# Splitting each scan step of a Mamba block into two halves of eight states

## The chip, the cores and the metric

The kernel runs on all 8 NeuronCores of one Trainium2 chip, each with two of the sixteen sequences. The time is that of the slowest core, in microseconds of the device, for one execution of the whole kernel. Lower is better.

## What is computed

A selective state-space (Mamba) block with a residual and a LayerNorm, and then a feed-forward block with a low-rank, token-dependent term, again with residual and LayerNorm. Model width is 1024, inner width 2048, 16 states for each inner channel, 2048 tokens in each sequence. The part that the change touches is the recurrence over the tokens:

```python
delta = softplus(xp[..., -1:] * w_dt + b_dt)
dA  = exp(delta[..., None] * A)                    # b, l, 2048, 16
dBx = (delta * xc)[..., None] * B_in[:, :, None, :]
def step(h, inp):
    dA_t, dBx_t, C_t = inp
    h = dA_t * h + dBx_t
    return h, einsum('bdn,bn->bd', h, C_t)         # y_t
y = ys + D_param * xc
y = y * silu(z)
return y @ W_out.T
```

## The kernel before

The kernel has three stages behind one another, with a barrier between them. The first casts and transposes the weights into scratch memory. The second, the scan phase, goes through 16 chunks of T = 256 tokens (8 for each of the core's two sequences). The third is the feed-forward block.

In the scan phase the 2048 inner channels are 16 groups of 128 partitions, and one group is a *step* here, counted 0 to 15 by `dt` in a chunk. The 16 states lie side by side in a row, so `dA`, `dbx` and `hc` are tiles of 128 x 4096 (16 states x 256 tokens). One scan instruction runs over several states in one go: the first column of `dA` of each state is set to zero, so that nothing is carried from one state into the next, and what the chunk before leaves over (`scar`) is put in by adding `dA * scar` to the first column of `dbx` (through `fixb`). In the first chunk of a sequence (k = 0) this pair of instructions is left out.

ScalarE (`emit_dA`, L702) makes `dA` with 16 `Exp` activations of 256 columns and then signals `dA_{jd}`. There are two `dA` buffers, and before it fills one it waits for `scan_{jd - 2}`. Its program is in one written-out order: behind step 0's `dA` the LayerNorm statistics of the chunk before; behind steps 2 to 5 four copies each of transposed input (L648) for the next chunk; behind steps 6 to 12 five or four evacuations each (`prep_evac`, L663 and L671), which wait for TensorE's products for the next chunk; ahead of step 8 the second half of `delta` (L693, L697); behind step 13 the evacuation of the B/C projection.

GpSimd multiplies `delta` by `xc` into `vv`, eight groups at a time (`vhalf`, L540), and signals `vH_{i}_{h}`, for which VectorE waits at steps 0 and 8. It also issues the chunk's loads and stores of its own queue. TensorE works on the next chunk's input projection and then on the output projection of the chunk before (`emit_wout_kt`), slab by slab as `ybuf` comes.

VectorE's step is a chain: wait for `dA`, `dbx` = `vv` x `brep` (L764), `fixb` (L772), add (L778), memset (L782), two scans over half of the row each (L786, L788) of which the second signals `scan_{jd}`, copy of the last column (L793), product with C (`crep`, L797), four adds that fold 16 states into one (L799 to L805), and the two instructions that make `ybuf` (L807, L811). Between instructions that depend on each other stands a `drain`. At the start of each chunk VectorE adds and normalizes the chunk before (L394, L412).

Of the kernel before, what the change touches and what calls it, by code (L numbers as in the profile page):

```python
# [8 lines left out]
FP16 = mybir.dt.float16  # L9
BF16 = mybir.dt.bfloat16  # L10
AF = mybir.ActivationFunctionType
OP = mybir.AluOpType

P = 128
# [4 lines left out]
NST = 16  # L19
H = 4096  # L20
T = 256
NCH = L // T
NDT = DIN // P
# [42 lines left out]
def build_nc(known_events=None, n_iters=B_LOC * NCH, do_a=True, do_b=True):  # L66
# [27 lines left out]
    ev = Ev(nc, known=known_events)  # L94
# [3 lines left out]
    a_sb = nc.alloc_sbuf_tensor("a_sb", [P, NDT * NST], F32)  # L98
# [238 lines left out]
    tsb = lambda nm, sh, dt: stA.enter_context(nc.sbuf_tensor(nm, sh, dt))  # L337
# [8 lines left out]
    vv = [tsb(f"vv{j}", [P, NDT * T], BF16) for j in range(2)]  # L346
    brep = [tsb(f"brep{j}", [P, NST * T], BF16) for j in range(2)]
    crep = [tsb(f"crep{j}", [P, NST * T], BF16) for j in range(2)]
    dtrep = [tsb(f"dtrep{j}", [P, T], F32) for j in range(2)]
    delta = [tsb(f"delta{j}", [P, T], F32) for j in range(8)]  # L350
    dA = [tsb(f"dA{j}", [P, NST * T], FP16) for j in range(2)]
    dbx = [tsb(f"dbx{j}", [P, NST * T], BF16) for j in range(2)]
    hc = tsb("hc", [P, NST * T], BF16)
    fixb = tsb("fixb", [P, NST], F32)
    scar = tsb("scar", [P, NDT * NST], F32)
# [10 lines left out]
    def it_bk(i):  # L366
        return i // NCH, i % NCH
# [88 lines left out]
    with nc.Block() as blk:  # L456
# [168 lines left out]
        def _(s):  # L625
# [74 lines left out]
                ev.mark(f"deltaH_{i}_{h}", "ac")  # L700

            def emit_dA(i, dt):  # L702
                jd = i * NDT + dt
                da_t = dA[jd % 2]
                if jd >= 2:
                    ev.wait(s, f"scan_{jd - 2}")
                for n in range(NST):
                    jx = s.activation(da_t[:, n * T:(n + 1) * T], delta[dt % 8][:],  # L708
                                      AF.Exp,
                                      scale=a_sb[:, dt * NST + n:dt * NST + n + 1])  # L710
                jx = ev.inc(jx, "ac", 1)
                ev.mark(f"dA_{jd}", "ac")

            if n_iters > 0:
                prep_tails(0)
# [33 lines left out]
        @blk.vector  # L749
        def _(v):  # L750
            ev.wait(v, "p0_params")
            for i in range(n_iters):
                b, k = it_bk(i)
                par = i % 2
                if i > 0:
                    emit_ln1_evac(v, i - 1)
                    emit_ln1_norm(v, i - 1)
                for dt in range(NDT):
                    if dt % 8 == 0:
                        ev.wait(v, f"vH_{i}_{dt // 8}")  # L760
                        ev.wait(v, f"zsil_{i}_{dt // 8 * 8 + 7}")
                    jd = i * NDT + dt
                    ev.wait(v, f"dA_{jd}")
                    jx = v.tensor_tensor(  # L764
                        dbx[jd % 2][:].rearrange("p (n t) -> p n t", n=NST),
                        vv[par][:, dt * T:(dt + 1) * T].unsqueeze(1)
                        .broadcast_to([P, NST, T]),
                        brep[par][:].rearrange("p (n t) -> p n t", n=NST),
                        OP.mult)
                    v.drain()  # L770
                    if k > 0:
                        jx = v.tensor_tensor(  # L772
                            fixb[:],
                            dA[jd % 2][:].rearrange("p (n t) -> p n t", n=NST)[:, :, 0],
                            scar[:, dt * NST:(dt + 1) * NST],
                            OP.mult)
                        v.drain()
                        jx = v.tensor_tensor(  # L778
                            dbx[jd % 2][:].rearrange("p (n t) -> p n t", n=NST)[:, :, 0],
                            dbx[jd % 2][:].rearrange("p (n t) -> p n t", n=NST)[:, :, 0],  # L780
                            fixb[:], OP.add)
                    jx = v.memset(dA[jd % 2][:]  # L782
                                  .rearrange("p (n t) -> p n t", n=NST)[:, :, 0:1], 0.0)
                    v.drain()
                    HT = NST * T // 2
                    jx = v.tensor_tensor_scan(hc[:, 0:HT], dA[jd % 2][:, 0:HT],  # L786
                                              dbx[jd % 2][:, 0:HT], 0.0, OP.mult, OP.add)
                    jx = v.tensor_tensor_scan(hc[:, HT:], dA[jd % 2][:, HT:],  # L788
                                              dbx[jd % 2][:, HT:], 0.0, OP.mult, OP.add)
                    jx = ev.inc(jx, "vc", 1)  # L790
                    ev.mark(f"scan_{jd}", "vc")
                    v.drain()  # L792
                    jx = v.tensor_copy(  # L793
                        scar[:, dt * NST:(dt + 1) * NST],
                        hc[:].rearrange("p (n t) -> p n t", n=NST)[:, :, T - 1])
                    v.drain()
                    jx = v.tensor_tensor(hc[:], hc[:], crep[par][:], OP.mult)  # L797
                    v.drain()
                    jx = v.tensor_add(hc[:, 0:8 * T], hc[:, 0:8 * T], hc[:, 8 * T:16 * T])  # L799
                    v.drain()  # L800
                    jx = v.tensor_add(hc[:, 0:4 * T], hc[:, 0:4 * T], hc[:, 4 * T:8 * T])  # L801
                    v.drain()
                    jx = v.tensor_add(hc[:, 0:2 * T], hc[:, 0:2 * T], hc[:, 2 * T:4 * T])
                    v.drain()
                    jx = v.tensor_add(hc[:, 0:T], hc[:, 0:T], hc[:, T:2 * T])  # L805
                    v.drain()
                    jx = v.scalar_tensor_tensor(gtmp[:], xc[par][:, dt * T:(dt + 1) * T],  # L807
                                                dp_sb[:, dt:dt + 1], hc[:, 0:T],
                                                OP.mult, OP.add)
                    v.drain()  # L810
                    jx = v.tensor_tensor(ybuf[par][:, dt * T:(dt + 1) * T], gtmp[:],  # L811
                                         zsil[par][:, dt * T:(dt + 1) * T], OP.mult)
                    jx = ev.inc(jx, "vc", 1)
                    ev.mark(f"ydt_{i}_{dt}", "vc")
                    v.drain()
                ev.mark(f"dloop_{i}", "vc")
            if n_iters > 0:
                emit_ln1_evac(v, n_iters - 1)
                emit_ln1_norm(v, n_iters - 1)
# [351 lines left out]
```

How the kernel before makes its waits and increments, by code:

```python
    def wait(self, eng, ev_name):  # L55
        tbl = self.known if self.known is not None else self.events
        if ev_name not in tbl:
            if self.known is not None:
                raise KeyError(f"unknown event {ev_name}")
            return
        sname, val = tbl[ev_name]
        if val > 0:
            eng.wait_ge(self.sem(sname), val)
# [183 lines left out]
            @blk.gpsimd  # L247
# [10 lines left out]
                            else:  # L258
                                ptag = JOBS[[jj[0] for jj in JOBS].index(tag) - 1][0]
                                if ptag == "ws":
                                    ev.wait(g, f"ws_sc{15 - (1 - r)}")
                                else:
                                    ev.wait(g, f"{ptag}_tr{(_prev_nr[ptag]) - (2 - r)}")
                        i = g.dma_start(out=wrow[r % 2][:, 0:cols],
                                        in_=src_ap[r * P:(r + 1) * P, :])
                        ev.inc(i, f"gw{r % 2}", 16)
                        ev.mark(f"{tag}_ld{r}", f"gw{r % 2}")
                g.wait_ge(ev.sem("gw0"), ev.cnt["gw0"])
                g.wait_ge(ev.sem("gw1"), ev.cnt["gw1"])
# [44 lines left out]
            @blk.sync  # L314
# [14 lines left out]
                    ev.mark(f"{tag}_alldoneA", "hd0")  # L329
                    ev.mark(f"{tag}_alldoneB", "hd1")
                sy.wait_ge(ev.sem("hd0"), ev.cnt["hd0"])
                sy.wait_ge(ev.sem("hd1"), ev.cnt["hd1"])
```

## Time and profile before

| | us |
|---|---|
| median of the timed runs (7847.22 and 7870.45) | 7858.83 |
| the profiled execution | 7886.68 |
| its span on the slowest core (core 2) | 7884.8 |
| spans of its eight cores | 7727.9 to 7884.8 |
| VectorE busy | 4727.9 |
| ScalarE busy | 3217.6 |
| TensorE matmul busy | 3936.6 |

All rows below are of core 2. The page of the profile gives the busy time of each engine (PE is TensorE, DVE is VectorE, ACT is ScalarE, POOL is GpSimd), and groups of instructions by line of the kernel. A row of a timeline gives the start in us from the span's start, the duration in us, the engine, the line, what is written from what, and in brackets how long the engine was idle just before and what ended that. "Issue" means that nothing in the profile ended it. A name with q behind the engine (POOLq) is that engine's sequencer.

### The profile page before, as it was taken

The numbers are of one execution on the slowest core, as the hardware profiler recorded it, in microseconds if no ns is written. First come the engines' busy times: TensorE is split into PE (matmuls) and PEld (weight loads), VectorE is DVE, ScalarE is ACT, GpSimd is POOL, SyncE is SP. The second block draws the span as 40 slices with busy tenths as digits, with TensorE's granted clock in tenths as the row PEclk, the third lists the DMA queues.
The fourth block names the chain that finished last, engine by engine and source line by source line (L and its number), as shares of the span: only waits on it lengthen the run. The fifth ranks groups of instructions, "written<-read, shape, count | busy, mean of one in ns | idle before, by whom it ended". The sixth has DMA issues, their size and how long they took to land.

```text
span 7884.8 us, 65714 instructions; the slowest of 8 cores (7727.9 to 7884.8 us)
## 1 busy us (share of the span) xinstructions
PE 3936.6 (50%) x18593; PEld 1984.5 (25%) x18720; DVE 4727.9 (60%) x3817; ACT 3217.6 (41%) x8279; POOL 474.9 (6%) x514
## 2 busy tenths in 40 slices
PE   4445353252542634426335263352500888868888
PEld 2213232131231412304223132131300222222223
DVE  1000488898889888898889898889986000000000
ACT  4443354554545545445455454554531222222221
POOL 0010010000100001000100010000101000010000
PEclk9999676575665666656656566565655777877777
DMA  3576242232322423224233242232303222333332
GB/s 82 112 125 153 82 129 83 68 109 68 108 87 64 119 69 100 88 59 130 77 83 98 58 129 76 75 99 62 115 16 56 77 79 85 96 82 102 102 96 91
DMA packets 591422, 707.86 MB, mean 90 GB/s; under 512 B 421359, under 2 KB 421359, under 8 KB 552160
## 3 DMA queue, kind: packets, MB, share of 16 engines
q1 hardware_dynamic: 561024, 608.48, 25.3%
q0 software_dynamic: 30048, 95.17, 6.7%
q8 instruction: 164, 2.69, 0.1%
q14 instruction: 186, 1.52, 0.1%
HBM read 707.33 MB, written 71.84 MB: 99 GB/s over the span
## 4 chain that ended last, share of the span: by engine, by line
DVE 28%; PE 24%; ACT 14%; DVEq 12%; DMA 7%; issue 4%; another core or an unknown queue 1%; ACTq 1%; POOL 0%; POOLq 0%; SPq 0%
DVE hc L786 11%; DVEq L792 11%; ACT dA L708 8%; PE ps_xz L586 7%; PE ps_h L974 7%; DVE dbx L764 6%; PE ps_oB L1006 5%; DVE hc L797 4%; DMA w1s_r<-win1s_scr 3%; DMA w_r<-w2T_scr 3%; DVE hc L799 2%; DVE hc L801 1%; PE ps_h L977 1%; ACT y1T L1043 1%
## 5 line engine op out<-in xcount | busy, mean ns | idle before, releaser
L708 ACT ACTIVATE dA<-delta,a_sb 128x256 f16<-128x256 f32 x4096 | 1662.2, 494 | 1234.0 <-DVE hc L788 1229.0
L586 PE MATMUL ps_xz<-xT,w1s_r 128*128 128x256 bf16 x8192 | 1154.2, 310 | 340.6 <-ACT xc L663 230.0
L786 DVE TENSOR_TENSOR_SCAN hc<-dA,dbx 128x2048 bf16<-128x2048 f16 x256 | 1132.8, 4425 | 19.5 <-issue 1.0
L788 DVE TENSOR_TENSOR_SCAN hc<-dA,dbx 128x2048 bf16<-128x2048 f16 x256 | 1133.0, 4426 | 0.0
L764 DVE TENSOR_TENSOR dbx<-vv,brep 128x4096 bf16<-128x4096 bf16 x256 | 586.9, 2293 | 836.6 <-ACT dA L708 784.6
L586 PEld LDWEIGHTS ps_xz<-xT,w1s_r 128*128 128x128 bf16 x8192 | 882.3, 110 | 580.1 <-issue 370.7
L379 PE MATMUL ps_wo<-wout_r,ybuf 128*128 128x512 bf16 x993 | 413.9, 568 | 1126.2 <-DVE ybuf L811 823.7
L571 PE MATMUL ps_tr<-ident,x_bf 128*128 128x128 bf16 x256 | 68.0, 266 | 1295.5 <-ACT xT L648 944.0
L602 PE MATMUL ps_xz<-xT,win_r 128*128 128x256 bf16 x2048 | 428.9, 390 | 410.1 <-ACT zsil L671 233.2
L797 DVE TENSOR_TENSOR hc<-hc,crep 128x4096 bf16<-128x4096 bf16 x256 | 592.9, 2316 | 20.8 <-issue 2.1
L1006 PE MATMUL ps_oB<-w_r,h_sb 128*128 128x512 bf16 x2000 | 551.9, 428 | 57.8 <-DMA w_r<-w2T_scr 37.7
L974 PE MATMUL ps_h<-y1T,w1t_sb 128*128 128x512 bf16 x2000 | 554.6, 424 | 16.3 <-DVE su_sb L1092 11.7
L540 POOL TENSOR_TENSOR vv<-delta,xc 128x256 bf16<-128x256 f32 x256 | 317.4, 1271 | 2787.8 <-ACT delta L697 2787.8
L379 PEld LDWEIGHTS ps_wo<-wout_r,ybuf 128*128 128x128 bf16 x1024 | 108.8, 121 | 1422.5 <-issue 1418.3
L1097 DVE TENSOR_SCALAR su_sb<-ps_ut,scl_sb 4x512 bf16<-4x512 f32 x32 | 23.6, 738 | 715.0 <-PE ps_ut L987 715.0
L1126 DVE TENSOR_TENSOR y2pre<-ps_oB,y1cb 128x512 f32<-128x512 f32 x64 | 44.3, 692 | 636.2 <-PE ps_oB L1022 634.4
L602 PEld LDWEIGHTS ps_xz<-xT,win_r 128*128 128x128 bf16 x2048 | 259.2, 133 | 574.4 <-issue 476.5
L663 ACT ACTIVATE xc<-ps_xz 128x256 bf16<-128x256 f32 x256 | 94.1, 382 | 751.0 <-PE ps_xz L590 750.4
L571 PEld LDWEIGHTS ps_tr<-ident,x_bf 128*128 128x128 bf16 x256 | 26.7, 104 | 1347.0 <-issue 1347.0
L1052 ACT ACTIVATE h_sb<-ps_h,b_sb 128x512 bf16<-128x512 f32 x256 | 175.9, 687 | 437.7 <-PE ps_h L977 437.4
L799 DVE TENSOR_TENSOR hc<-hc 128x2048 bf16<-128x2048 bf16 x256 | 320.8, 1253 | 19.4 <-issue 0.4
L307 ACT COPY p_stage<-p_psa 128x128 bf16<-128x128 bf16 x704 | 186.6, 265 | 340.5 <-PE p_psa L241 318.0
(115 smaller groups left out, 3844.0 us busy)
## 6 DMA issues: line engine op xcount, KB each, us to landing
w1s_r<-win1s_scr SPq DMA_DIRECT2D x256, 1024.0 KB, 5.0
w_r<-w2T_scr SPq DMA_DIRECT2D x512, 256.0 KB, 3.1
win_r<-winT_scr SPq DMA_DIRECT2D x256, 256.0 KB, 2.9
wout_r<-woutT_scr SPq DMA_DIRECT2D x256, 256.0 KB, 3.3
win1s_scr<-p_stage SPq DMA_DIRECT2D x64, 256.0 KB, 2.4
brep<-bc_scr POOLq DMA_DIRECT2D x16, 1024.0 KB, 9.4
crep<-bc_scr POOLq DMA_DIRECT2D x16, 1024.0 KB, 14.0
out<-outsb SPq DMA_DIRECT2D x32, 512.0 KB, 4.0
```

The lines of the kernel that those rows point to most:

```text
L379: jx = t.matmul(ps_wo[grp][:], ybuf[par][:, kt * T + tM * P:kt * T + (tM + 1) * P], wout_ring[jj % 2][:, nh * 512:(nh + 1) * 512], start=( ...
L586: jx = t.matmul(pst[:], w1s_ring[jj % 2][:, (k4 * NKD + kt) * P:(k4 * NKD + kt + 1) * P], xT[par][:, kt * TE + 1 + k4:kt * TE + 1 + k4 + T ...
L602: jx = t.matmul(pst[:], win_ring[jj % 2][:, kt * P:(kt + 1) * P], xT[par][:, kt * TE + 4:kt * TE + 4 + T], start=(kt == 0), stop=(kt == NK ...
L708: jx = s.activation(da_t[:, n * T:(n + 1) * T], delta[dt % 8][:], AF.Exp, scale=a_sb[:, dt * NST + n:dt * NST + n + 1])
L764: jx = v.tensor_tensor(dbx[jd % 2][:].rearrange("p (n t) -> p n t", n=NST), vv[par][:, dt * T:(dt + 1) * T].unsqueeze(1) .broadcast_to([P, ...
L786: jx = v.tensor_tensor_scan(hc[:, 0:HT], dA[jd % 2][:, 0:HT], dbx[jd % 2][:, 0:HT], 0.0, OP.mult, OP.add)
L788: jx = v.tensor_tensor_scan(hc[:, HT:], dA[jd % 2][:, HT:], dbx[jd % 2][:, HT:], 0.0, OP.mult, OP.add)
L792: v.drain()
L797: jx = v.tensor_tensor(hc[:], hc[:], crep[par][:], OP.mult)
L799: jx = v.tensor_add(hc[:, 0:8 * T], hc[:, 0:8 * T], hc[:, 8 * T:16 * T])
L974: jx = t.matmul(pst[:], w1t_sb[:, kt * H + m * P:kt * H + (m + 1) * P], y1T[par][:, kt * TB:(kt + 1) * TB], start=(kt == 0), stop=False)
L1006: jx = t.matmul(ps_o[gq][:], h_sb[:, kt * TB + tM * P:kt * TB + (tM + 1) * P], w2_ring[jj % 4][:, nh * 512:(nh + 1) * 512], start=(kt == 0 ...
```

## The change

The tiles `dA` and `dbx` become half as wide (8 states, 128 x 2048) and twice as many (4 instead of 2). ScalarE signals after each eight activations, and waits before each half for the scan that last read the same buffer. VectorE runs the part of the step from `dbx` to the scan twice, once for each half, each with a wait of its own for its half of `dA` and a signal behind its scan. The part of the step from the copy of the last column on stays as it is, on the whole row of `hc`.

```diff
--- before.py
+++ after.py
@@ -348,8 +348,8 @@
     crep = [tsb(f"crep{j}", [P, NST * T], BF16) for j in range(2)]
     dtrep = [tsb(f"dtrep{j}", [P, T], F32) for j in range(2)]
     delta = [tsb(f"delta{j}", [P, T], F32) for j in range(8)]
-    dA = [tsb(f"dA{j}", [P, NST * T], FP16) for j in range(2)]
-    dbx = [tsb(f"dbx{j}", [P, NST * T], BF16) for j in range(2)]
+    dA = [tsb(f"dA{j}", [P, 8 * T], FP16) for j in range(4)]
+    dbx = [tsb(f"dbx{j}", [P, 8 * T], BF16) for j in range(4)]
     hc = tsb("hc", [P, NST * T], BF16)
     fixb = tsb("fixb", [P, NST], F32)
     scar = tsb("scar", [P, NDT * NST], F32)
@@ -700,16 +700,18 @@
                 ev.mark(f"deltaH_{i}_{h}", "ac")
 
             def emit_dA(i, dt):
-                jd = i * NDT + dt
-                da_t = dA[jd % 2]
-                if jd >= 2:
-                    ev.wait(s, f"scan_{jd - 2}")
-                for n in range(NST):
-                    jx = s.activation(da_t[:, n * T:(n + 1) * T], delta[dt % 8][:],
-                                      AF.Exp,
-                                      scale=a_sb[:, dt * NST + n:dt * NST + n + 1])
-                jx = ev.inc(jx, "ac", 1)
-                ev.mark(f"dA_{jd}", "ac")
+                for nh in range(2):
+                    jh = (i * NDT + dt) * 2 + nh
+                    da_t = dA[jh % 4]
+                    if jh >= 4:
+                        ev.wait(s, f"scan_{jh - 4}")
+                    for n8 in range(8):
+                        n = nh * 8 + n8
+                        jx = s.activation(da_t[:, n8 * T:(n8 + 1) * T], delta[dt % 8][:],
+                                          AF.Exp,
+                                          scale=a_sb[:, dt * NST + n:dt * NST + n + 1])
+                    jx = ev.inc(jx, "ac", 1)
+                    ev.mark(f"dA_{jh}", "ac")
 
             if n_iters > 0:
                 prep_tails(0)
@@ -759,37 +761,38 @@
                     if dt % 8 == 0:
                         ev.wait(v, f"vH_{i}_{dt // 8}")
                         ev.wait(v, f"zsil_{i}_{dt // 8 * 8 + 7}")
-                    jd = i * NDT + dt
-                    ev.wait(v, f"dA_{jd}")
-                    jx = v.tensor_tensor(
-                        dbx[jd % 2][:].rearrange("p (n t) -> p n t", n=NST),
-                        vv[par][:, dt * T:(dt + 1) * T].unsqueeze(1)
-                        .broadcast_to([P, NST, T]),
-                        brep[par][:].rearrange("p (n t) -> p n t", n=NST),
-                        OP.mult)
-                    v.drain()
-                    if k > 0:
+                    jh0 = (i * NDT + dt) * 2
+                    for nh in range(2):
+                        jh = jh0 + nh
+                        ev.wait(v, f"dA_{jh}")
                         jx = v.tensor_tensor(
-                            fixb[:],
-                            dA[jd % 2][:].rearrange("p (n t) -> p n t", n=NST)[:, :, 0],
-                            scar[:, dt * NST:(dt + 1) * NST],
+                            dbx[jh % 4][:].rearrange("p (n t) -> p n t", n=8),
+                            vv[par][:, dt * T:(dt + 1) * T].unsqueeze(1)
+                            .broadcast_to([P, 8, T]),
+                            brep[par][:, nh * 8 * T:(nh + 1) * 8 * T]
+                            .rearrange("p (n t) -> p n t", n=8),
                             OP.mult)
                         v.drain()
-                        jx = v.tensor_tensor(
-                            dbx[jd % 2][:].rearrange("p (n t) -> p n t", n=NST)[:, :, 0],
-                            dbx[jd % 2][:].rearrange("p (n t) -> p n t", n=NST)[:, :, 0],
-                            fixb[:], OP.add)
-                    jx = v.memset(dA[jd % 2][:]
-                                  .rearrange("p (n t) -> p n t", n=NST)[:, :, 0:1], 0.0)
-                    v.drain()
-                    HT = NST * T // 2
-                    jx = v.tensor_tensor_scan(hc[:, 0:HT], dA[jd % 2][:, 0:HT],
-                                              dbx[jd % 2][:, 0:HT], 0.0, OP.mult, OP.add)
-                    jx = v.tensor_tensor_scan(hc[:, HT:], dA[jd % 2][:, HT:],
-                                              dbx[jd % 2][:, HT:], 0.0, OP.mult, OP.add)
-                    jx = ev.inc(jx, "vc", 1)
-                    ev.mark(f"scan_{jd}", "vc")
-                    v.drain()
+                        if k > 0:
+                            jx = v.tensor_tensor(
+                                fixb[:, nh * 8:nh * 8 + 8],
+                                dA[jh % 4][:].rearrange("p (n t) -> p n t", n=8)[:, :, 0],
+                                scar[:, dt * NST + nh * 8:dt * NST + nh * 8 + 8],
+                                OP.mult)
+                            v.drain()
+                            jx = v.tensor_tensor(
+                                dbx[jh % 4][:].rearrange("p (n t) -> p n t", n=8)[:, :, 0],
+                                dbx[jh % 4][:].rearrange("p (n t) -> p n t", n=8)[:, :, 0],
+                                fixb[:, nh * 8:nh * 8 + 8], OP.add)
+                        jx = v.memset(dA[jh % 4][:]
+                                      .rearrange("p (n t) -> p n t", n=8)[:, :, 0:1], 0.0)
+                        v.drain()
+                        jx = v.tensor_tensor_scan(hc[:, nh * 8 * T:(nh + 1) * 8 * T],
+                                                  dA[jh % 4][:], dbx[jh % 4][:],
+                                                  0.0, OP.mult, OP.add)
+                        jx = ev.inc(jx, "vc", 1)
+                        ev.mark(f"scan_{jh}", "vc")
+                        v.drain()
                     jx = v.tensor_copy(
                         scar[:, dt * NST:(dt + 1) * NST],
                         hc[:].rearrange("p (n t) -> p n t", n=NST)[:, :, T - 1])
```

## Rows read from the trace of the kernel before

**Rows 1.** The page, part 1: busy us (share of the span) xinstructions

```profile
PE 3936.6 (50%) x18593; PEld 1984.5 (25%) x18720; DVE 4727.9 (60%) x3817; ACT 3217.6 (41%) x8279; POOL 474.9 (6%) x514
```

**Rows 2.** One chunk: us, busy of PE, PEld, DVE, ACT, POOL; PEclk, DMA, GB/s

```profile
2825.76:3147.59 321.83, 133.40 (x750) 82.89 (x752) 288.81 (x230) 157.81 (x379) 25.36 (x22) 0.62 0.30 89
```

**Rows 3.** Waits, all of the span: us in total, times, longest us

```profile
DVE dbx L764 <- ACT dA L708: 784.6, 73, 648.0
...
DVE dbx L764 <- POOLq L543: 17.6, 9, 2.2
...
DVE x_bf L412 <- ACT lncol L448: 113.7, 16, 7.3
...
ACT dA L708 <- DVE hc L788: 1229.0, 134, 14.1
```

**Rows 4.** Timeline of VectorE, step 9: start us, us [idle before <-releaser]

```profile
3001.64 2.29 DVE L764 TENSOR_TENSOR dbx<-vv,brep 128x4096 bf16<-128x4096 bf16 x1 [5.63 <-ACT dA L708]
3004.00 0.18 DVE L772 TENSOR_TENSOR fixb<-dA,scar 128x16 f32<-128x16 f16 x1
3004.26 0.23 DVE L778 TENSOR_TENSOR dbx<-dbx,fixb 128x16 bf16<-128x16 bf16 x1
3004.49 0.07 DVE L782 MEMSET dA<- 128x16 f16 x1
3004.63 4.42 DVE L786 TENSOR_TENSOR_SCAN hc<-dA,dbx 128x2048 bf16<-128x2048 f16 x1
3008.97 4.40 DVE L788 TENSOR_TENSOR_SCAN hc<-dA,dbx 128x2048 bf16<-128x2048 f16 x1
3013.46 0.18 DVE L793 CAST scar<-hc 128x16 f32<-128x16 bf16 x1
...
3020.16 2.29 DVE L764 TENSOR_TENSOR dbx<-vv,brep 128x4096 bf16<-128x4096 bf16 x1 [0.16 <-issue]
```

**Rows 5.** Timeline of VectorE, first instruction of steps 4 and 8

```profile
2899.94 2.29 DVE L764 TENSOR_TENSOR dbx<-vv,brep 128x4096 bf16<-128x4096 bf16 x1 [0.16 <-ACT xT L648]
...
2977.64 2.29 DVE L764 TENSOR_TENSOR dbx<-vv,brep 128x4096 bf16<-128x4096 bf16 x1 [1.61 <-POOLq L543]
```

**Rows 6.** Timeline of ScalarE, `dA` of steps 6, 7 and 9

```profile
2911.77 6.49 ACT L708 ACTIVATE dA<-delta,a_sb 128x256 f16<-128x256 f32 x16 [9.58 <-DVE hc L788]
...
2936.75 6.50 ACT L708 ACTIVATE dA<-delta,a_sb 128x256 f16<-128x256 f32 x16
...
2995.05 6.49 ACT L708 ACTIVATE dA<-delta,a_sb 128x256 f16<-128x256 f32 x16
```

**Rows 7.** Line L799, and L764's group: durations ns min/median/max; busy, mean ns

```profile
L799 DVE TENSOR_TENSOR hc<-hc x256: 1224/1226/1693, 905.1 to 6033.3; 128x2048 bf16<-128x2048 bf16 x128
...
L764 DVE TENSOR_TENSOR dbx<-vv,brep 128x4096 bf16<-128x4096 bf16 x256 | 586.9, 2293 | 836.6 <-ACT dA L708 784.6
```

**Rows 8.** Timeline of VectorE, a step of the first chunk

```profile
909.17 2.29 DVE L764 TENSOR_TENSOR dbx<-vv,brep 128x4096 bf16<-128x4096 bf16 x1 [0.16 <-ACT xT L648]
911.62 0.07 DVE L782 MEMSET dA<- 128x16 f16 x1 [0.16 <-issue]
...
920.60 0.17 DVE L793 CAST scar<-hc 128x16 f32<-128x16 bf16 x1
```

**Rows 9.** Timeline of VectorE, step 7: a pause that nothing ended

```profile
2967.96 2.29 DVE L797 TENSOR_TENSOR hc<-hc,crep 128x4096 bf16<-128x4096 bf16 x1 [0.43 <-issue]
```

**Rows 10.** Timeline of GpSimd, the two halves of `vv`

```profile
2968.84 8.35 POOL L540 TENSOR_TENSOR vv<-delta,xc 128x256 bf16<-128x256 f32 x8 [138.20 <-ACT delta L697]
...
3101.42 13.27 POOL L540 TENSOR_TENSOR vv<-delta,xc 128x256 bf16<-128x256 f32 x8 [35.65 <-ACT delta L697]
```

**Rows 11.** Timeline of VectorE, step 14, beside the second of these

```profile
3094.60 2.29 DVE L764 TENSOR_TENSOR dbx<-vv,brep 128x4096 bf16<-128x4096 bf16 x1 [0.16 <-ACT dA L708]
...
3101.93 4.83 DVE L788 TENSOR_TENSOR_SCAN hc<-dA,dbx 128x2048 bf16<-128x2048 f16 x1
...
3115.63 2.29 DVE L764 TENSOR_TENSOR dbx<-vv,brep 128x4096 bf16<-128x4096 bf16 x1 [0.16 <-issue]
```

## The prediction, made before the changed kernel was run

> **What bounds the kernel now.** I read the busy table of the page first, then the waits, then one chunk of the scan phase on both engines. Over the whole span VectorE is busy 60% and ScalarE 41% [rows 1]; the scan phase is where the two meet. There one chunk of 256 tokens lasts 321.8 us, and VectorE works in 288.8 us of it against ScalarE's 157.8 us [rows 2]. So VectorE sets the pace, and the waits show what is left to win: before the first instruction of a step (L764) it sat 784.6 us waiting for `dA`, of which one wait of 648.0 us is the start of the phase; the other 72 sum to 136.6 us. Another 17.6 us went to GpSimd (nine waits). ScalarE in turn waited 1229.0 us for the scans at L788 [rows 3]. Nearly everywhere ScalarE is ahead, and its waiting costs nothing.
>
> **Where VectorE's waits fall.** An undisturbed step (one `dt`, 128 channels) takes 18.52 us from L764 to L764 [rows 4]. In the chunk read here, step 8 starts 77.70 us behind step 4 (2899.94 to 2977.64), where 4 x 18.52 are 74.1: 3.6 us late, 1.6 of them idle on GpSimd; step 9 starts another 5.5 us late (3001.64), idle on ScalarE [rows 4, 5]. The cause stands on ScalarE: from step 6's `dA` (2911.77) to step 7's (2936.75) pass 25.0 us, of which 6.5 are `dA` and the rest are table loads and evacuations paced by TensorE; step 9's `dA` begins at 2995.05 and ends at 3001.5, just before VectorE starts [rows 6]. Three such ScalarE steps of over 18.52 us eat a lead that elsewhere is large.
>
> **What the change adds.** I take the first step of [rows 4]: L764 at 3001.64 to L793 at 3013.46 is 11.82 us. After the change this stretch is two halves, each with its own `dbx`, `fixb`, add, memset and one scan.
> - A half-size `dbx`: no row, but L799 is the same operation on the same 128x2048 shape, 1.226 us median [rows 7]; the full one is 2.29 [rows 4], 2.293 to three places [rows 7].
> - One half: 1.23 + 0.07 gap + 0.18 + 0.08 gap + 0.23 + 0.07 + 0.07 gap + 4.42 + 0.09 gap = 6.44 us. The gap behind the first scan also holds a wait; the gap at L764 with a satisfied wait is 0.16 rather than 0.09, so 0.07 more. Sum: 6.44 + 6.44 + 0.07 = 12.95 us, which is 1.13 more. In it, the two scans lose the 0.08 us by which they overlap now (4.42 long, 4.34 apart).
> - The four small instructions work on 8 columns instead of 16. Bounds: no shrinking (1.13) and, at a column per ns as the full scan and `dbx` rows suggest at most, some 0.05 less (1.08). I take 1.10.
> - In the first chunk of each of the two sequences (32 steps) there is no `fixb` pair. There the stretch is 909.17 to 920.60, 11.43 us, with a 0.16 gap ahead of the memset [rows 8]; two halves of 1.23 + 0.16 + 0.07 + 0.07 + 4.42 + 0.09 = 6.04 and 0.07 make 12.15, 0.72 more; I take 0.70.
> - 224 x 1.10 + 32 x 0.70 = 246 + 22 = 269 us. The scans stay 512 of 4.42 us. None of this lies beside other VectorE work: it is the busy engine, so all of it is on the path outside the waits.
> - VectorE shows pauses of 0.36 us beyond the usual gap now and then, released by nothing (one at L797) [rows 9]; I count about 2.3 per chunk. With a third more instructions in the stream: 16 x 2.3 x 0.36 x 0.35 = 5 us. Total added: 274 us. With the durations known only this well, I allow 245 to 300.
>
> On the price of one more instruction a page stands against the row. The Trainium skill (VectorE: DVE Perf Modes, "The TRN2 errata") tables the fixed part of a VectorE instruction as 58 cycles at 0.96 GHz, 60 ns, and says that it is exposed between instructions, so that many small tiles pay it each time. The rows give 2 x 1.226 - 2.293 = 0.159 us for one more `dbx`, and they decide; by the table the `dbx` term alone would be 256 x 0.060 = 15 us instead of 41.
>
> **What it removes.** ScalarE may refill a half as soon as that half's scan is done. In the pace of VectorE, `dA` of step 6 starts 11.83 us behind the start of step 4 (2899.94 to 2911.77) [rows 5, 6] and ends at +18.3. After, its second half starts at about +12.9 and takes 3.25, ending at +16.1: 2.2 us earlier. VectorE's steps are 1.1 longer, so step 9 comes 5 x 1.1 = 5.5 us later against step 4 once its own delays are set aside. And step 9 may start on a first half, 3.25 us earlier still; the second half is asked for only 6.5 us behind that. In the sample chunk `dA` of step 9 is 9.1 us late in total against undelayed steps; the three reliefs sum to 10.9, and the slowdown by GpSimd (below) gives 2 more. So this wait goes. The wait at step 8 is for GpSimd's product `vv`, which follows the second `delta` half; it too comes 2.2 earlier and is asked for 4.4 later, but GpSimd then works wholly beside VectorE and needs longer: 13.27 us as at 3101.42, against 8.35 at 2968.84 where VectorE stood idle at the end [rows 10]. `vv` starts 50.6 us behind the end of step 6's `dA`, so at +66.7 behind step 4, and ends at +80.0; VectorE arrives at 4 x 19.63 = 78.5 plus what `vv` slows it, about 80.5. Just hidden.
>
> Gain: 136.6 + 17.6 = 154 us, less the ordinary gap of 0.16 that is part of each of 81 waits (13) = 141. Beside `vv`, one step takes 21.03 us instead of 18.52 (3094.60 to 3115.63; L788 takes 4.83 instead of 4.40) [rows 4, 11]. Now the late `vv` slows step 7 by some 1.7 us before VectorE goes idle; after, by the full 2.5: 15 x 0.8 = 12 us back. In about three of 15 chunks ScalarE is 4 us later than in this sample, for which I leave 8 us of waits. Gain: 121 us; bounds 60 (half the waits stay) and 154.
>
> Not moved: at each chunk's end VectorE waits for TensorE's last slab and for the LayerNorm statistics (113.7 us, sixteen times) [rows 3], behind the last step either way. SP's and GpSimd's queues get no new DMA. The buffers hold as many bytes. What is late next after the removed wait is VectorE itself.
>
> **The sum.** 274 - 121 = +153 us. Against the profiled execution, 7886.7 us, that is 8040; that execution lies 28 us above the median of the runs, 7858.8, so the forecast is 8012 us, 1.9% slower. A difference of 2% (157 us) is about the least that counts as a change here, and 8016 is that line: the forecast sits on its near side by very little.
>
> **Rivals.**
> - *A, the waits mostly stay.* If ScalarE's chain through steps 6 to 9 stretches with TensorE's evacuations, the lead won at step 6 is lost and half of the waits remain: 274 - 60 = +214, 8073 us. For it: the chain is paced by TensorE. Against: the longer steps alone give 4.4 us by step 8. Chance 0.14.
> - *B, GpSimd becomes the wait.* If each product in `vv` waits for a whole VectorE instruction, and more scans of 4.42 us lie in its stretch than at 3101.42, `vH` is late at step 8 in every chunk by up to 4.9 us (13.27 - 8.35): 15 x 4.9 = 74, 8086 us. For it: L788 at 3101.93 and the instructions behind it are each about 0.3 longer while `vv` runs [rows 10, 11]. Chance 0.12. The Trainium skill (SBUF, State Buffer, "Who interferes with whom") says the two engines share one port pair, held for a whole instruction while the other blocks; the trace agrees in kind, 13.27 against 8.35 us.
> - *C, faster: added instructions hide.* The kernel gets faster if a split step costs less than 121/256 = 0.47 us more, that is if small instructions run within the gaps and tails of their neighbours. If each of the four more instructions costs no more than a gap, 0.07, it is 0.28: 72 - 121 = -49, 7810 us. Against: the busy time of the four, 0.159 + 0.18 + 0.23 + 0.07 = 0.64, is above the point already, and their rows stand one behind another with gaps [rows 4]. Chance 0.05.
> - The forecast, 7960 to 8050: chance 0.68, of it 0.46 below 8016. Anything else 0.01.
>
> Range 7960 to 8090, which leaves out C and the last part of A and B. Faster by over 2% 0.01, within 2% 0.51 (0.46 + 0.05), slower 0.48 (0.22 + 0.14 + 0.12).
>
> **What would show it.** In the profile after: an undisturbed step of 19.6 us; `dbx` 512 times at 1.23; a second scan 6.5 us behind the first; waits of `dbx` for `dA` below some 20 us beyond the first one; ScalarE starting each half 3.3 us or more ahead; the step beside `vv` still 2.5 us longer; phases ahead of and behind the scans unchanged. A step of under 19.2 or over 20.0 us, or waits above 60 us, would make the prediction wrong.

## The result, and the profile after

The changed kernel takes 7996.1 us, median of its runs, against 7873.9 us for the kernel before, in runs that stand beside each other. The ratio is 1.0204, with a 95% interval of 1.0141 to 1.0266: slower, by an amount that lies on both sides of 2%. In some executions of either kernel, the profiled one of the kernel before among them, the cores of one die show a lower granted clock (there 0.686, core 2 among them, against 0.733 on the other die) and take over 1% longer; the ratio is of executions without this, and so it is not the 1.0155 of the two medians. The sections below compare stretches of the traces, which scatter far less than the whole. The profiled execution took 8017.2 us; its span was 8014.5 us on core 3, all of whose rows are shown unless another core is named.

The page of the changed kernel, part 5 (columns: line, engine, operation, tiles, count | busy us, mean ns | idle before and its releaser):

```profile
L790 DVE TENSOR_TENSOR_SCAN hc<-dA,dbx 128x2048 bf16<-128x2048 f16 x512 | 2271.8, 4437 | 39.5 <-issue 2.3
...
L768 DVE TENSOR_TENSOR dbx<-vv,brep 128x2048 bf16<-128x2048 bf16 x512 | 630.2, 1231 | 735.5 <-POOLq L543 648.7
```

The same 512 scans as before, and 512 `dbx` instead of 256: 630.2 us in place of 586.9 us [rows 7]. One step of the timeline of VectorE, step 9 of chunk 6 (counted from 0, as in [rows 4]):

```profile
3044.18 1.23 DVE L768 TENSOR_TENSOR dbx<-vv,brep 128x2048 bf16<-128x2048 bf16 x1 [0.16 <-issue]
3045.48 0.17 DVE L777 TENSOR_TENSOR fixb<-dA,scar 128x8 f32<-128x8 f16 x1
3045.72 0.19 DVE L783 TENSOR_TENSOR dbx<-dbx,fixb 128x8 bf16<-128x8 bf16 x1
3045.89 0.07 DVE L787 MEMSET dA<- 128x8 f16 x1
3046.03 4.43 DVE L790 TENSOR_TENSOR_SCAN hc<-dA,dbx 128x2048 bf16<-128x2048 f16 x1
3050.61 1.23 DVE L768 TENSOR_TENSOR dbx<-vv,brep 128x2048 bf16<-128x2048 bf16 x1 [0.16 <-issue]
3051.91 0.17 DVE L777 TENSOR_TENSOR fixb<-dA,scar 128x8 f32<-128x8 f16 x1
3052.16 0.20 DVE L783 TENSOR_TENSOR dbx<-dbx,fixb 128x8 bf16<-128x8 bf16 x1
3052.32 0.07 DVE L787 MEMSET dA<- 128x8 f16 x1
3052.46 4.42 DVE L790 TENSOR_TENSOR_SCAN hc<-dA,dbx 128x2048 bf16<-128x2048 f16 x1
3056.98 0.18 DVE L796 CAST scar<-hc 128x16 f32<-128x16 bf16 x1
...
3063.68 1.23 DVE L768 TENSOR_TENSOR dbx<-vv,brep 128x2048 bf16<-128x2048 bf16 x1 [0.16 <-issue]
```

This answers to [rows 4]. The stretch from the first `dbx` to the copy of the last column is now 12.80 us (3044.18 to 3056.98) where it was 11.82 us, and the undisturbed step is 19.50 us where it was 18.52. In the first chunk of a sequence it is 18.80 us, where it was 18.13.

The waits over the whole span (us in total, times, longest us; lines are left out):

```profile
ACT dA L710 <- DVE hc L790: 1297.6, 269, 11.3
...
DVE dbx L768 <- POOLq L543: 648.7, 12, 643.8
...
DVE dbx L768 <- ACT dA L710: 1.8, 6, 1.0
```

Against [rows 3]: of the waits for `dA` 1.8 us are left, and of the 648.7 us for GpSimd 643.8 are the single wait at the start of the phase. The eleven others sum to 4.9 us: nine are the usual gap of 0.30 us, and 0.67 and 1.54 us are the only two that are longer. What VectorE lost in steps 8 and 9 is gone, and its chain of instructions alone sets the pace.

ScalarE's timeline in the same chunk, in which step 4 starts at 2943.79 on VectorE:

```profile
2950.16 3.31 ACT L710 ACTIVATE dA<-delta,a_sb 128x256 f16<-128x256 f32 x8 [7.30 <-DVE hc L790]
2956.94 3.31 ACT L710 ACTIVATE dA<-delta,a_sb 128x256 f16<-128x256 f32 x8 [3.47 <-DVE hc L790]
...
2978.87 6.52 ACT L710 ACTIVATE dA<-delta,a_sb 128x256 f16<-128x256 f32 x16
...
3036.97 6.52 ACT L710 ACTIVATE dA<-delta,a_sb 128x256 f16<-128x256 f32 x16
```

The two halves for step 6 start 6.4 and 13.2 us behind the start of step 4; the second ends at 2960.25, 16.5 us behind it, where the whole tile ended 18.3 us behind it before [rows 5, 6]. Of these 16.5 us 0.35 are a pause of VectorE that nothing ended, of the kind in [rows 9], between the two scans of step 4. Step 9's `dA` starts at 3036.97 and is complete at 3043.49, 0.7 us ahead of VectorE's 3044.18.

Steps 7 and 8 on VectorE, and then GpSimd's two halves of `vv`:

```profile
3002.61 1.23 DVE L768 TENSOR_TENSOR dbx<-vv,brep 128x2048 bf16<-128x2048 bf16 x1 [0.16 <-issue]
...
3024.68 1.23 DVE L768 TENSOR_TENSOR dbx<-vv,brep 128x2048 bf16<-128x2048 bf16 x1 [0.30 <-POOLq L543]
...
3011.98 12.12 POOL L540 TENSOR_TENSOR vv<-delta,xc 128x256 bf16<-128x256 f32 x8 [141.68 <-ACT delta L697]
...
3145.32 15.57 POOL L540 TENSOR_TENSOR vv<-delta,xc 128x256 bf16<-128x256 f32 x8 [38.97 <-ACT delta L697]
```

The step beside `vv` takes 22.07 us instead of 19.50; a pause of 0.36 us of the kind in [rows 9] is part of it, and the instruction behind the pause is not slowed. In eight other chunks, without that pause, it takes 22.03 us. Step 8 then starts with a gap of 0.30 us, the same as at a chunk's start, where several satisfied waits stand and nothing is late; so `vv` is in time. GpSimd needs 12.12 and 15.57 us for eight products, against 8.35 and 13.27 before [rows 10].

How much the scan phase grew depends on the core. From its first `dbx` to the end of its last normalization, on cores 2 and 5 of the kernel before (columns: window, length, busy us and count of PE, PEld, DVE, ACT, POOL, then granted clock, DMA share, GB/s):

```profile
891.01:6050.58 5159.57, 2063.38 (x11313) 1261.30 (x11344) 4597.02 (x3616) 2476.43 (x5929) 368.20 (x338) 0.61 0.28 84
...
880.69:6001.31 5120.62, 1928.82 (x11344) 1203.63 (x11344) 4606.81 (x3616) 2475.94 (x5929) 393.75 (x338) 0.65 0.29 84
```

And on cores 0, 3 and 5 of the changed kernel:

```profile
883.69:6159.99 5276.30, 2011.45 (x11344) 1236.83 (x11344) 4754.10 (x4576) 2491.97 (x5931) 490.18 (x338) 0.62 0.27 82
...
887.24:6163.91 5276.67, 1939.40 (x11344) 1204.78 (x11344) 4753.07 (x4576) 2501.23 (x5931) 481.13 (x338) 0.64 0.28 82
...
896.36:6172.38 5276.02, 1929.39 (x11344) 1207.49 (x11344) 4753.74 (x4576) 2491.81 (x5931) 484.80 (x338) 0.65 0.27 82
```

Before, a core at a granted clock of 0.61 in this stretch took 5159.6 us and one at 0.65 took 5120.6 us. After, at 0.62, 0.64 and 0.65, all three took 5276. So the phase grew by some 117 us at the low clock (117.1 us from slowest core to slowest core), but by 155.4 us on core 5, at the same clock of 0.65. That core 3 ended last is not the scan phase's doing: what lies behind it takes 1850.6 us on core 3 and 1720.8 us on core 0. The reason for the two sizes of growth is in the waits of core 5 before, which VectorE had less of than core 2 did [rows 3]:

```profile
DVE dbx L764 <- ACT dA L708: 732.6, 78, 639.7
...
DVE dbx L764 <- POOLq L543: 15.7, 13, 1.6
```

Without the start (639.7 us) these are 92.9 and 15.7 us, 108.6 together, against 154.2 us on core 2. The chain on ScalarE that made VectorE late waits for TensorE's products, 750.4 us in all at L663 on core 2 and 713.5 us on core 5, and it is longer where the clock is lower. No run changes the clock alone; this rests on the comparison of cores. The change removes nearly all of VectorE's waits, much or little, and adds the same instructions everywhere.

### The profile page after: what moved, and what is told of

The parts are those of the page before. It is cut to its first block, busy times and chain, and to the rows that moved or that the text cites. A ratio compares the mean times of both kernels' runs of the same rounds, so it can differ in the third digit from the quotient of the medians.

```text
span 8014.5 us, 68303 instructions; the slowest of 8 cores (7880.8 to 8014.5 us)
## 1 busy us (share of the span) xinstructions
PE 3807.4 (48%) x18720; PEld 1924.4 (24%) x18720; DVE 4884.7 (61%) x4777; ACT 3243.9 (40%) x8279; POOL 587.4 (7%) x514
## 4 chain that ended last, share of the span: by engine, by line
DVE 52%; PE 19%; DMA 6%; ACT 6%; issue 5%; DVEq 2%; another core or an unknown queue 1%; ACTq 0%; POOL 0%; POOLq 0%; SPq 0%
DVE hc L790 25%; DVE dbx L768 7%; PE ps_h L977 7%; DVE hc L800 6%; PE ps_oB L1009 4%; DVE hc L802 3%; DMA w_r<-w2T_scr 3%; PE ps_xz L586 3%; DVE hc L804 2%; DMA w1s_r<-win1s_scr 2%; ACT dA L710 2%; DVE gtmp L810 1%; DVE hc L806 1%; DVE ybuf L814 1%; PE ps_h L980 1%
## 5 line engine op out<-in xcount | busy, mean ns | idle before, releaser
L710 ACT ACTIVATE dA<-delta,a_sb 128x256 f16<-128x256 f32 x4096 | 1683.5, 497 | 1302.8 <-DVE hc L790 1297.6
L586 PE MATMUL ps_xz<-xT,w1s_r 128*128 128x256 bf16 x8192 | 1069.6, 294 | 412.2 <-ACT xc L663 249.2
L768 DVE TENSOR_TENSOR dbx<-vv,brep 128x2048 bf16<-128x2048 bf16 x512 | 630.2, 1231 | 735.5 <-POOLq L543 648.7
L586 PEld LDWEIGHTS ps_xz<-xT,w1s_r 128*128 128x128 bf16 x8192 | 840.3, 105 | 612.6 <-issue 439.8
L540 POOL TENSOR_TENSOR vv<-delta,xc 128x256 bf16<-128x256 f32 x256 | 430.0, 1711 | 2827.0 <-ACT delta L697 2827.0
L602 PE MATMUL ps_xz<-xT,win_r 128*128 128x256 bf16 x2048 | 408.3, 376 | 429.0 <-ACT zsil L671 237.6
L663 ACT ACTIVATE xc<-ps_xz 128x256 bf16<-128x256 f32 x256 | 94.6, 384 | 728.0 <-PE ps_xz L590 727.3
L1066 ACT ACTIVATE lnjB<-y2pre 128x1024 f32<-128x1024 f32 x32 | 33.7, 1054 | 712.4 <-DVE y2pre L1129 712.3
```

What stands on the lines that cost most here:

```text
L540: j = g.tensor_tensor(vv[par][:, dt * T:(dt + 1) * T], delta[dt % 8][:], xc[par][:, dt * T:(dt + 1) * T], OP.mult)
L586: jx = t.matmul(pst[:], w1s_ring[jj % 2][:, (k4 * NKD + kt) * P:(k4 * NKD + kt + 1) * P], xT[par][:, kt * TE + 1 + k4:kt * TE + 1 + k4 + T ...
L602: jx = t.matmul(pst[:], win_ring[jj % 2][:, kt * P:(kt + 1) * P], xT[par][:, kt * TE + 4:kt * TE + 4 + T], start=(kt == 0), stop=(kt == NK ...
L710: jx = s.activation(da_t[:, n8 * T:(n8 + 1) * T], delta[dt % 8][:], AF.Exp, scale=a_sb[:, dt * NST + n:dt * NST + n + 1])
L768: jx = v.tensor_tensor(dbx[jh % 4][:].rearrange("p (n t) -> p n t", n=8), vv[par][:, dt * T:(dt + 1) * T].unsqueeze(1) .broadcast_to([P, 8 ...
```

## Experiments

The length that is compared below is that of 14 chunks, from the first `dbx` of chunk 1 to that of chunk 15: 4529.3 us before on core 2, 4492.1 us before on core 5, 4627.1 and 4627.9 us after (cores 3 and 5). Over the cores it is 4526.7 to 4530.5 us before on cores 0 to 3, 4483.5 to 4492.1 us before on cores 4 to 7, and 4626.3 to 4628.5 us after on all eight. The clocks given with a core below are means over its whole span unless the phase is named.

### Split on VectorE, whole signals on ScalarE

```diff
-                    if jh >= 4:
-                        ev.wait(s, f"scan_{jh - 4}")
+                    if jh >= 4 and nh == 0:
+                        ev.wait(s, f"scan_{jh - 3}")
...
-                    jx = ev.inc(jx, "ac", 1)
-                    ev.mark(f"dA_{jh}", "ac")
+                    if nh == 1:
+                        jx = ev.inc(jx, "ac", 1)
+                        ev.mark(f"dA_{jh - 1}", "ac")
+                        ev.mark(f"dA_{jh}", "ac")
```

> VectorE's instructions as in the changed kernel, two halves with four more small instructions; ScalarE signals dA and refills its tiles only in pairs, as whole tiles, as before. Theory (the longer steps cost 0.97 us each whatever the signals do, and the waits go because of both the longer steps and the finer signals): an undisturbed step of 19.49 us, and waits of VectorE for dA only partly gone, since a chunk's relief at step 9 is 5 x 0.97 less 1.0 for the later refill = 3.9 us of the 9 to 11 that are needed: 60 to 100 us of waits left, sum +170 to +200 us against before. Rival (longer steps alone cover the waits, the finer signals do nothing): waits under 20 us and the same +118 us over the scan phase as the changed kernel.

Measured: ratio 1.0225 (1.0144 to 1.0305). The undisturbed step is 19.49 us and the 14 chunks take 4669.4 us on core 5 (granted clock 0.726 over its span), 177 us more than the kernel before on its core 5 and 41.5 us more than the changed kernel. Core 5 is the slowest; the others take from 4647.1 us on. The waits of core 5:

```profile
DVE dbx L770 <- ACT dA L710: 706.2, 69, 651.0
...
DVE dbx L770 <- POOLq L543: 12.8, 15, 2.2
```

55.2 us for `dA` besides the start, and 12.8 us for GpSimd, usual gaps included. For `dA` that is less than the 60 to 100 us that were expected, and on the other cores it is less still, down to 32.6 us. Over the whole phase core 5 takes 5325.0 us, 204 us more than the 5120.6 us before, and the core with the shortest phase takes 5300.0 us, 179 us more, so that the +170 to +200 of the theory holds nearly. The rival falls: some waits are left on every core, and the 14 chunks are 20 to 42 us longer than in the changed kernel. Longer steps alone take away part of the waits, 108.6 down to 68.0 us on core 5 and to about 40 us on the cores with the least, and the finer signals take the rest. They are worth 20 to 42 us here and don't pay for the instructions that they need.

### Refill by halves, VectorE's instructions as before

```diff
-                if jd >= 2:
-                    ev.wait(s, f"scan_{jd - 2}")
                 for n in range(NST):
+                    if jd >= 2 and n % 8 == 0:
+                        ev.wait(s, f"scan_{jd - 2}_{n // 8}")
...
                     jx = v.tensor_tensor_scan(hc[:, 0:HT], dA[jd % 2][:, 0:HT],
                                               dbx[jd % 2][:, 0:HT], 0.0, OP.mult, OP.add)
+                    jx = ev.inc(jx, "vc", 1)
+                    ev.mark(f"scan_{jd}_0", "vc")
...
```

(the signal behind the second scan is now `scan_{jd}_1`)

> VectorE's instructions as before; only a signal behind the first scan is added, and ScalarE refills each half of a dA tile as soon as the scan over that half is done. Theory: step 18.52 us, dA of a step ends 3.2 us earlier behind the scans that it waits for, so about 3.2 us of wait a chunk go: 80 to 110 us of the 141 stay, -45 us against before, ratio 0.994. Rival (it is the early refill that removes the waits in the changed kernel): waits under 20 us, -120 us, ratio 0.985.

Measured: ratio 0.9937 (0.9895 to 0.9979), the step 18.52 us, 14 chunks 4452.5 us on core 7 (clock 0.715 over its span) and 4444.2 us on core 0 (0.732), 40 to 48 us less than the kernel before on its core 5. Waits of core 7, the slowest:

```profile
DVE dbx L764 <- ACT dA L708: 692.8, 15, 646.9
...
DVE dbx L764 <- POOLq L543: 5.5, 13, 1.6
```

45.9 us for `dA` besides the start. Core 5 of the same execution, at a granted clock of 0.62 in the phase where core 7 had 0.64, has more of them, and its 14 chunks take 4480.0 us:

```profile
DVE dbx L764 <- ACT dA L708: 725.1, 17, 648.9
...
DVE dbx L764 <- POOLq L543: 14.3, 13, 2.2
```

76.2 us for `dA` and 14.3 us for GpSimd, usual gaps included, and some 86 us without them. The ratio is as expected. The 80 to 110 us of waits had been worked out from core 2 before, at 0.61; core 5 here is at the lower end of them, and core 7 below. The rival (under 20 us) falls on every core. One signal more, and no instruction: this half of the change is a small gain by itself, clear of the noise.

### Three `dA` buffers, one `dbx`

```diff
-    dA = [tsb(f"dA{j}", [P, NST * T], FP16) for j in range(2)]
-    dbx = [tsb(f"dbx{j}", [P, NST * T], BF16) for j in range(2)]
+    dA = [tsb(f"dA{j}", [P, NST * T], FP16) for j in range(3)]
+    dbx = [tsb(f"dbx{j}", [P, NST * T], BF16) for j in range(1)]
...
-                if jd >= 2:
-                    ev.wait(s, f"scan_{jd - 2}")
+                if jd >= 3:
+                    ev.wait(s, f"scan_{jd - 3}")
```

(with `dA[jd % 3]` for the tile and `dbx[0]` in the loop)

> Whole tiles as before, three dA buffers instead of two and one dbx instead of two (VectorE alone writes and reads dbx), so the same bytes. Theory (what the change gained was lead of ScalarE, which buffers give without more instructions): step 18.52 us, ScalarE up to a whole step further ahead, waits for dA and vv under 15 us, the step beside vv 21.0 us: -120 to -130 us over the scan phase, ratio 0.984. Rival (TensorE's evacuations set the pace of steps 6 to 9 whatever the lead): 60 us or more of waits stay, ratio 0.992 or above.

Measured: ratio 0.9894 (0.9851 to 0.9936). 14 chunks take 4413.2 us on core 4 (clock 0.694 over its span) and 4412.5 us on core 1 (0.731), and 4412.4 to 4413.7 us on all eight: the phase has become independent of the clock. Against the kernel before that is 116 us less than its core 2 and 79 us less than its core 5. The waits of core 4:

```profile
DVE dbx L764 <- ACT dA L708: 652.5, 46, 645.2
```

Of 652.5 us 645.2 are the start; the other 45 waits are the usual gaps. No wait for GpSimd is left. The lead that the change bought with instructions is to be had with buffers, in the same bytes. The rival falls. The expected 0.984 was too much, again because it was worked out from the waits of core 2. The whole phase on core 4, at a granted clock of 0.61 in it:

```profile
888.90:5924.29 5035.39, 2064.37 (x11344) 1263.22 (x11344) 4614.46 (x3616) 2473.22 (x5929) 437.34 (x338) 0.61 0.29 86
```

That is 124 us less than core 2 before took at the same clock and 85 us less than core 5, where the theory said 120 to 130.

### The changed kernel with a whole `dbx`

```diff
-                        jx = v.tensor_tensor(
-                            dbx[jh % 4][:].rearrange("p (n t) -> p n t", n=8),
...
+                        dbw = dbx[(jh // 2) % 2]
+                        dbh = dbw[:, nh * 8 * T:(nh + 1) * 8 * T]
+                        if nh == 0:
+                            jx = v.tensor_tensor(
+                                dbw[:].rearrange("p (n t) -> p n t", n=NST),
...
```

(`dbx` is two whole tiles again, and the add and the scan take the half `dbh`)

> The changed kernel with dbx made by one instruction over the whole row, everything else in halves. Theory (one more dbx costs 2 x 1.23 - 2.29 = 0.17 and a gap of 0.07): step 19.49 - 0.24 = 19.25 us, waits as in the changed kernel, -61 us against it, so about +57 us over the scan phase against before. Rival (an instruction costs 0.06 us of its own, the rest overlaps): step 19.4 us, -16 us against the changed kernel.

Measured: ratio 1.0131 (1.0078 to 1.0184), 14 chunks 4576.6 us, 50.5 us less than the changed kernel; over the whole phase it is 56 us (5220.9 us on core 1, the slowest), where 61 were expected. A step of its timeline:

```profile
2873.81 2.29 DVE L771 TENSOR_TENSOR dbx<-vv,brep 128x4096 bf16<-128x4096 bf16 x1 [0.16 <-issue]
2876.18 0.17 DVE L779 TENSOR_TENSOR fixb<-dA,scar 128x8 f32<-128x8 f16 x1
...
2881.31 0.17 DVE L779 TENSOR_TENSOR fixb<-dA,scar 128x8 f32<-128x8 f16 x1 [0.16 <-issue]
...
2886.38 0.18 DVE L798 CAST scar<-hc 128x16 f32<-128x16 bf16 x1
...
2893.07 2.29 DVE L771 TENSOR_TENSOR dbx<-vv,brep 128x4096 bf16<-128x4096 bf16 x1 [0.16 <-issue]
```

The step is 19.26 us (2873.81 to 2893.07), 0.24 less, as expected: one more `dbx` costs 0.17 us of busy time and a gap of 0.07. The rival of 0.06 us for one more instruction falls. 0.24 of the 0.97 us is `dbx`, and the rest is the second `fixb`, add and memset with their gaps, and the gap between the scans.

### Without `vv`, on the kernel with three buffers

```diff
-                    for dt in range(h * 8, h * 8 + 8):
+                    for dt in range(h * 8, h * 8 + (8 if i < 2 else 0)):
```

> The kernel with three dA buffers, but GpSimd makes vv only for the first two chunks and later chunks use these again (so the output is not the reference's). Theory (each of the eight products of a half holds up one VectorE instruction by about 0.31 us, and nothing else is waited for): from the third chunk on the step of 21.03 us is 18.52, and the two slowed steps in the middle (20.3 and 19.2) are 18.52 too: 14 x 5.0 = -70 us of scan phase against the kernel with three buffers, 4413 to 4348 us for its 14 chunks. Rival (the slower steps come from something else that runs then, such as ScalarE's or the DMA queues' traffic): they stay at 21.03 and 20.3.

This kernel was timed in one execution. With three buffers and `vv`, the step beside its first half for the next chunk, on core 4 (VectorE's timeline):

```profile
3020.34 2.29 DVE L764 TENSOR_TENSOR dbx<-vv,brep 128x4096 bf16<-128x4096 bf16 x1 [0.16 <-ACT dA L708]
...
3027.68 4.83 DVE L788 TENSOR_TENSOR_SCAN hc<-dA,dbx 128x2048 bf16<-128x2048 f16 x1
...
3041.37 2.29 DVE L764 TENSOR_TENSOR dbx<-vv,brep 128x4096 bf16<-128x4096 bf16 x1 [0.16 <-issue]
```

21.03 us. The same step without `vv`, on core 4 as well:

```profile
2998.16 2.29 DVE L764 TENSOR_TENSOR dbx<-vv,brep 128x4096 bf16<-128x4096 bf16 x1 [0.16 <-ACT dA L708]
...
3016.68 2.29 DVE L764 TENSOR_TENSOR dbx<-vv,brep 128x4096 bf16<-128x4096 bf16 x1 [0.16 <-ACT dA L708]
```

18.52 us. The 14 chunks take 4346.9 us, 66.3 us less than 4413.2 us, where 65 were forecast (the second half of chunk 1's `vv` is still made in chunk 1); over the whole phase it is 68.9 us, where 70 were forecast. From chunk 2 on the slowed steps in the middle of a chunk are gone too. So the slower step is GpSimd's doing, and it is 2.51 us for eight products, 0.31 us for each. The rival falls.

### Normalization behind step 0, with three buffers

```diff
                 if i > 0:
                     emit_ln1_evac(v, i - 1)
-                    emit_ln1_norm(v, i - 1)
                 for dt in range(NDT):
+                    if i > 0 and dt == 1:
+                        emit_ln1_norm(v, i - 1)
```

> Three dA buffers, and VectorE normalizes the chunk before behind step 0 instead of ahead of it, so that ScalarE's statistics run beside step 0. Theory: the 7.1 us that VectorE waits at each chunk's end for the statistics go (15 times), the distance from step 15 to the next step 0 falls from 31.96 to about 24.9 us (with the normalization's 1.5 in step 0 instead, 23.4), -106 us against the kernel with three buffers, ratio to before 0.976. Rival (the later normalization delays the next chunk's input and TensorE's transposes, and ScalarE comes late for steps 3 to 9): waits for dA of 30 us or more appear and half of the gain is gone.

Measured: ratio 0.9713 (0.9642 to 0.9784), median 7575.2 us. The end of a chunk on VectorE's timeline:

```profile
2724.78 2.29 DVE L765 TENSOR_TENSOR dbx<-vv,brep 128x4096 bf16<-128x4096 bf16 x1 [0.16 <-issue]
...
2745.37 2.48 DVE L394 TENSOR_TENSOR y1pre<-ps_wo,x_bf 128x512 f32<-128x512 f32 x4 [2.23 <-PE ps_wo L379]
2748.16 2.29 DVE L765 TENSOR_TENSOR dbx<-vv,brep 128x4096 bf16<-128x4096 bf16 x1 [0.30 <-issue]
...
2766.81 1.54 DVE L412 TENSOR_SCALAR x_bf<-y1pre,lncol 128x1024 bf16<-128x1024 f32 x2 [0.28 <-issue]
2768.51 2.29 DVE L765 TENSOR_TENSOR dbx<-vv,brep 128x4096 bf16<-128x4096 bf16 x1 [0.16 <-issue]
```

From the last step's `dbx` to the next chunk's are 23.38 us, against 31.96 us with the normalization ahead of it; 1.8 us of this come back in step 0, where the normalization (L412) no longer waits. The 14 chunks take 4316.1 us (4315.9 to 4317.0 us over the cores), 97 us less than with three buffers alone (106 were expected, for 15 chunk ends; here it is 6.9 us at each of 14, where 7.1 were expected). No new wait for `dA` appears, so the rival falls. Over the whole phase it is 104 us; the ratio fell by more, 0.018 or some 140 us, which the width of the two intervals can hold. By its median this is the fastest version that was run, faster than the kernel before and than the changed one.

### Evacuation moved as well

```diff
-                    if dt == 0 and i > 0:
+                    if dt == 1 and i > 0:
                         emit_lnstat(s, i - 1)
...
                 if i > 0:
-                    emit_ln1_evac(v, i - 1)
+                    pass
                 for dt in range(NDT):
                     if i > 0 and dt == 1:
+                        emit_ln1_evac(v, i - 1)
+                    if i > 0 and dt == 2:
                         emit_ln1_norm(v, i - 1)
```

> As the kernel with the late normalization, but the evacuation of the output projection too is moved behind step 0, the statistics behind step 1's dA, and the normalization behind step 1. Theory: the 2.2 us wait for TensorE's last slab at each chunk's end goes as well, -33 us more, ratio to before 0.972. Rival: the next chunk's input now lands some 46 us into the chunk, ScalarE waits for its transposes ahead of step 3's dA, and the waits that appear are larger than the 2.2 us that go.

Measured: ratio 0.9767 (0.9695 to 0.9839), which can't be told from the version before it. The 14 chunks take 4300.1 us on core 4 (4296.8 to 4305.9 us over the cores), 16 us less than 4316.1 us, half of what was expected. The 2.2 us wait for TensorE is gone at each chunk's end, but step 2 of nearly every chunk now takes 19.0 to 19.5 us instead of 18.52, with waits of mostly 0.5 to 1.0 us for `dA` where 0.16 is the usual gap: the rival happens in part.

## Why the prediction came out as it did

The forecast was 8012 us against 7858.8 us, a ratio of 1.0195; measured is 1.0204. That closeness is in good part luck: against core 5, whose growth is the like of the measured one, two terms of the sum, the added instructions and the removed waits, were each off by some 36 us, in opposite directions.

*What bounds the kernel.* Right. VectorE sets the pace of the scan phase; three buffers take its waits for `dA` and `vv` away and leave 18.52 us for an undisturbed step, and nothing else moved in.

*The added instructions.* The sum had 1.10 us for a step, 0.70 in the first chunk of a sequence, 274 us in all. Measured are 0.97 and 0.67: 224 x 0.97 + 32 x 0.67 = 239 us. The kernel with three buffers, which has the old instructions and no such waits, gives it once more without any sum over steps: 5276.3 - 5035.4 = 241 us. The term that was mis-sized is the small instructions on 8 columns. The `dbx` (1.23), the gaps and the scans are as worked out, and the experiment with a whole `dbx` gives its 0.24. But the add (L783) is followed by the memset after 0.16 to 0.17 us instead of 0.23, where I had allowed at most 8 ns for the eight columns fewer. The lower bound of 1.08 was therefore no bound, and neither was the 245 of the allowance of 245 to 300 us.

*The removed waits.* On core 2 they were 141 us without the usual gaps, and 121 us was the gain that I expected. At that core's clock, 0.61 in the phase, the phase grew by 117 us, so the gain was 239 - 117 = 122 us: on the core that the prediction had read, the step is right in size and in place, and the whole sum of +153 us is 36 us too high there. On core 5, at 0.65, the gain was 239 - 155 = 84 us, and there the two errors (35 us in the instructions, 37 us in the waits) cancel. The kernel with three buffers gives the same two sizes, 124 and 85 us. The 1.0204 of the timed runs is 161 us, near the 155 of core 5. The prediction took the waits of one core as those of the kernel, and it was a core with a low clock, where core 5 of the same execution waited 108.6 us.

*What took the waits away.* Two of the three reliefs of the prediction are shown by the first two experiments, with all waits for `dA` and GpSimd counted, usual gaps included: longer steps alone left 68.0 us on the slowest core, the early refill alone 51.4 us on core 7 and 90.5 us on core 5, at a lower clock in the phase, and both with the early start left next to none (6.7 us). The 3.25 us from starting on a first half was not needed in the chunk shown, as step 9's whole `dA` was complete in time; no run takes it away alone. The end of step 6's `dA` came 1.8 us earlier against step 4, and without the pause of 0.35 us it is the forecast 2.2.

*GpSimd.* Rival B's mechanism exists: with more scans in its stretch the chunk-end half of `vv` took 15.57 us instead of 13.27. But the half that step 8 needs took 12.12 us and came in time in the chunk shown, and in all but two of the others; "just hidden" held. The step beside it was 2.5 us longer in most chunks (22.03 against 19.49), as forecast. The Trainium skill (SBUF, State Buffer, "Who interferes with whom") has the two engines share a port pair, which one holds for a whole instruction while the other blocks. The trace agrees in kind: VectorE's step is longer only while `vv` runs, and the experiment without `vv` removes exactly that. In size it is less than a whole instruction of GpSimd: the shortest product lasts 0.66 us (L540), and each costs VectorE 0.31 us.

*Rival A* (half of the waits stay) and *rival C* (added instructions hide) both fell: A by the waits after, 1.8 and 4.9 us, C by the whole-`dbx` experiment, which priced one more instruction and its gap at 0.24 us. The Trainium skill's table (VectorE: DVE Perf Modes, "The TRN2 errata") would have made the `dbx` term 15 us; the rows after give 630.2 - 586.9 = 43.3 us of busy time, near the 41 us of the prediction. The measurement decides, and the same section says below its table that the 58 cycles are too few and the measured fixed part is about 150 cycles, an estimate of 0.156 us at its 0.96 GHz; the rows, with 0.159 us, agree.

*What was not predicted.* That the scan phase after would take the same time at every clock (5276.3, 5276.7 and 5276.0 us at 0.62, 0.64 and 0.65). It follows from the argument: what VectorE still waits for TensorE, at each chunk's end (L394), was the same before on cores 2 and 5, 35.7 and 35.9 us, and is 36.1 to 36.2 us after on all three cores. But the prediction didn't draw it.

## What to carry to other kernels

As these runs have it: when the busy engine waits a few us for a producer that is usually far ahead, give the producer more lead by another buffer or by a signal that needs no instruction, before splitting the consumer's work: the split is paid in every step, the wait was paid in two of sixteen. Here one `dbx` buffer too many was the room for a third `dA`. And before a removed wait is priced, read it on all cores: a wait that ends on TensorE's work was larger on the cores with the lower clock (154.2 against 108.6 us), the price of the added instructions was the same on all.

## What the runs showed of the hardware

- An in-place add on 128x8 bf16 elements, one element every 512 bytes, let the next instruction start 0.065 us earlier than one on 128x16 (0.165 against 0.23 us from start to start), 8 ns for each column and not 1. The first of the pair (`fixb`, L772 and L777) saved only about 0.01 us.
- Each product of GpSimd (128x256, bf16 from f32 and bf16) held up VectorE by 0.31 us in all, whether scans of 4.4 us or adds of 0.3 us ran beside it (4.83 for 4.40, 0.60 for 0.29), and the products themselves took as long as VectorE's instructions let them: 8.35 us for eight with VectorE idle at the end, 15.57 us with the rest of one scan and a whole second one in the stretch.
